# A graph network on one core: the node jobs of the background all ahead of its slot jobs, one every four groups

## The chip, the cores and the metric

The kernel runs on one core of one Trainium2 chip. The metric is device time in microseconds (us) of one execution, the median of the runs shown. PE is TensorE (PEld its weight loads), DVE is VectorE, ACT is ScalarE, POOL is GpSimd and SP is SyncE, which here only issues DMAs. L12 is line 12 of the kernel before; in the changed kernel the same code stands up to seven lines lower.

## The reference

50,000 nodes have 96 features each, and 25,000 edges join them. The edges are sorted by `dst`. Four layers follow one another, each under a residual sum and a layer norm:

```python
edge_index = jnp.stack([src, dst])
x = _layernorm(x + _L0(x, edge_index, edge_attr_17, ...))   # edge network, sum over dst
x = _layernorm(x + _L1(x, edge_index))                      # K = 10 times: out = spmm(out) * 0.9 + h * 0.1
x = _layernorm(x + _L2(x, edge_index))                      # K = 16 times: normalized sum over neighbours
x = _layernorm(x + _L3(x, edge_index, W1, b1, W2, b2, prelu_a))  # twice: x @ W, sum, + b, prelu
```

Most rows of the result hang on few edges or on none. A node without edges needs in layer 3 only its own row: two products with the 96x96 weights, two prelus and a norm.

## The kernel before, in words

**The passes.** After a preparation of some 1,280 us, `passes` runs four stages: "power" (layer 1, K1 = 10 passes), "smooth" (layer 2, K2 = 16 passes), and the two convolutions "conv1" and "conv2" of one pass each. A pass handles the 25,088 edge slots in NGP = 49 groups of 512 rows. For each group g POOL issues four indirect DMAs of 128 rows each (the gathers, L1823) into one of RG = 7 buffers `l_g`. PE transposes them (`turn`, L1850), DVE runs the segmented sum over the 512 columns (`scan`, L2007), PE turns the sums of group g - 2 back (`turn_back`, L1876 in power; L1858 and L1867 in smooth), DVE makes the new rows (L2050 and L2059 or L2063 in power; L2032 and L2050 in smooth), and SP stores them in a table (L2228). In the first pass of power and of smooth ACT scales the gathered rows first (`prepare`, L1922), and PE's `turn` waits for that. In power's ninth pass (p = 8) DVE does three operations in place of the one of L2063 (L2070, L2071, L2072).

**What POOL waits for.** Ahead of the gathers of group q it waits until PE's step q - 7 is done, since they write that group's buffer, and until the gathers of group q - 2 have landed. Ahead of a pass it waits until every row of the pass before is stored. In that gap it does other work where there is some: in power passes 2 to 9 up to 25 gathers of other rows (L1806), and in smooth a lot of finished rows.

**The background.** Beside power and smooth runs a second, independent piece of work, the class `Tail`: layer 3 for nodes and slots that need no neighbours. It has 149 jobs: 100 node jobs (500 nodes each, 125 rows on the partitions, loaded from `x3d`, stored in the output) and 49 slot jobs (512 slots each, loaded from `x3t`, stored in `outc` and partly in `h1t`). A job is a chain over all engines, and each of its links stands at a fixed offset. `background` calls `turn` once for each group 1 to 40 of every pass but a stage's last. These calls are the "slots", 40 a pass, 360 in power and 600 in smooth; slot s stands at group s % 40 + 1, on PE ahead of that group's own `turn`, on DVE and ACT behind that group's own work. A job that begins at slot b has:

- SP loads the rows at b (L227) and stores the result at b + 12
- PE transposes at b + 1 (L253); ACT copies at b + 2 (L261); PE multiplies at b + 3 (L266); ACT rectifies at b + 4 (L274, L275); DVE merges at b + 5 (L280); PE multiplies at b + 6 (L289); ACT rectifies at b + 7 (L307, L308); DVE merges at b + 8 (L314, L316); PE transposes back at b + 9 (L326)
- DVE takes the statistics at b + 10 (L338 to L345), ACT their root at b + 10 (L353); DVE inverts at b + 11 (L363, L364), ACT scales the rows at b + 11 (L373)

Each link waits on a semaphore for the one before. All queues run in order, so an engine that waits for a link holds back what is behind it, the work of the pass too. `PERIOD` = 6: job n begins at slot 6n. The order of the jobs is 60 node jobs, 49 slot jobs, 40 node jobs.

**The lots.** The rows that the slot jobs stored are scattered to the output in 19 lots of 2 to 4 groups, four indirect DMAs each group (`send_lot`, L1780). SP loads a lot into one of two tiles, of which the second is `lots[1]`. One lot goes out ahead of each smooth pass 1 to 15, two behind smooth's last gathers and two behind conv1's. A lot of 2 groups is 8 scatters, one of 3 groups 12.

Of the kernel before, what the change touches and what calls it, by code (L numbers as in the profile page):

```python
# [46 lines left out]
PERIOD = 6  # L47
# [66 lines left out]
class Tail:  # L114


    def __init__(self, prog, s):
# [11 lines left out]
        self.up, self.down = tmp("up", [D, GE]), tmp("down", [D, GE])  # L129
# [138 lines left out]
    def rectify_first(self, act, n):  # L268
        w = U * self.parts(n)
        self.seen(act, n, 3)  # L270
        if n:
            self.seen(act, n - 1, 9)
        a, z = self.nc.scalar, self.p.bank[5][0:D, 0:w]
        a.activation(self.up[:, 0:w], z, ACT.Relu, bias=self.p.c1[:, 0:1])  # L274
        a.activation(self.down[:, 0:w], z, ACT.Relu, bias=self.p.c1n[:, 0:1], scale=-1.0).then_inc(self.rect1, 1)  # L275

    def merge_first(self, dve, n):
        w = U * self.parts(n)
        dve.wait_ge(self.rect1, n + 1)
        self.nc.vector.scalar_tensor_tensor(out=self.up[:, 0:w], in0=self.down[:, 0:w], scalar=self.p.neg[:, 0:1],  # L280
                                            in1=self.up[:, 0:w], op0=ALU.mult, op1=ALU.add).then_inc(self.merged1, 1)

    def mult_second(self, pe, n):
# [2007 lines left out]
```

## Time and profile before

| | |
|---|---|
| time, median of 3 runs | 9357.71 us (9357.03 to 9362.42) |
| the profiled execution, span | 9366.9 us |
| PE busy | 5546.5 us (59%), 23638 instructions |
| DVE busy | 4843.1 us (52%) |
| ACT busy | 2149.1 us (23%) |
| POOL busy | 6850.8 us (73%), 7074 instructions |
| DMA | 957.89 MB, mean 102 GB/s |
| mean granted TensorE clock | 0.635 of full speed |

Power's first gather starts at 1284.8 us, smooth's at 4337.0 us, conv1's at 8571.1 us. The groups of instructions give for each line its count, its busy time, the mean of one, and the idle time of the engine ahead of it with what ended it; the timeline gives single instructions in order of time. An instruction behind "x4" is four in a row, given with their common length. PE's times are those of a pipeline, so one instruction may start before the other's end.

### The profile page before, as it was taken

How to read it: one execution, taken by the hardware profiler on the slowest of the kernel's cores; microseconds unless marked ns; L12 is line 12 of the kernel's file. 1: busy time of each engine (PE TensorE's matmuls, PEld its weight loads, DVE VectorE, ACT ScalarE, POOL GpSimd, SP SyncE). 2: the span in 40 equal slices, each digit the busy share in tenths (PEclk: the TensorE clock that was granted, in tenths of full speed). 3: DMA queues.
4: the chain of work that ended last, by engine and by line, in shares of the span. 5: the costliest groups of instructions: out<-in, count | busy, mean ns of one | idle time of the engine just before them, and what ended most of it. 6: DMA issues, size and time to landing. Idle time of an engine off the chain costs nothing. (4 is left out here: it accounts for less than half of the span.)

```text
span 9366.9 us, 86355 instructions
## 1 busy us (share of the span) xinstructions
PE 5546.5 (59%) x23638; PEld 4458.1 (48%) x23638; DVE 4843.1 (52%) x12040; ACT 2149.1 (23%) x5791; POOL 6850.8 (73%) x7074
## 2 busy tenths in 40 slices
PE   7565754444443444313777777777777777676643
PEld 6455642233222232202665666656555665555643
DVE  7666644454444456643555555555555554455454
ACT  2366542011000011331211111111111110046433
POOL 6554767777777777767777777777777777777777
PEclk9655655555555555556777777777777777666565
DMA  7555353343333343432444444444444443333311
GB/s 144 130 166 162 80 97 96 98 107 98 97 97 96 98 106 97 111 83 70 112 107 109 114 112 108 110 109 104 104 105 102 107 108 97 94 96 87 90 46 37
DMA packets 909306, 957.89 MB, mean 102 GB/s; under 512 B 370946, under 2 KB 799320, under 8 KB 908726
## 3 DMA queue, kind: packets, MB, share of 16 engines
q1 hardware_dynamic: 652854, 588.49, 20.9%
q0 software_dynamic: 225792, 323.35, 18.3%
q10 hardware_dynamic: 30178, 40.53, 1.2%
q8 instruction: 191, 3.13, 0.1%
q14 instruction: 291, 2.38, 0.1%
HBM read 561.02 MB, written 418.54 MB: 105 GB/s over the span
## 5 line engine op out<-in xcount | busy, mean ns | idle before, releaser
L1823 POOL DMA_INDIRECT l_g<-tab,l x2940 | 2844.3, 967 | 917.0 <-issue 865.7
L2007 DVE TENSOR_TENSOR_SCAN l_w<-l_m,l_w,bank 96x512 f32<-96x512 bf16 x1248 | 1592.3, 1276 | 2890.7 <-PE bank L1850 2884.8
L1850 PE MATMUL bank<-ident,l_g 128*96 128x128 f32 x5096 | 1200.2, 381 | 2368.9 <-DMA l_g<-tab,XM 1080.2
L1850 PEld LDWEIGHTS bank<-ident,l_g 128*96 128x96 f32 x5096 | 780.5, 174 | 2858.4 <-DMA l_g<-tab,XM 1207.0
L1823 POOL DMA_INDIRECT l_g<-tab,XM x1764 | 1723.6, 977 | 550.0 <-issue 511.5
L1867 PEld LDWEIGHTS bank<-ident,l_w 96*128 96x128 f32 x6272 | 1602.9, 328 | 324.2 <-issue 253.4
L1867 PE MATMUL bank<-ident,l_w 96*128 96x96 f32 x6272 | 1505.2, 400 | 8.2 <-DVE l_w L2007 7.9
L1858 PE MATMUL bank<-XM,ident 128*128 128x384 f32 x1568 | 921.6, 681 | 0.0
L353 ACT ACTIVATE tail_sc<-tail_mv,eps_x 125x4 f32<-125x4 f32 (+1 forms) x149 | 44.3, 297 | 3404.5 <-DVE tail_mean L345 3404.5
L1876 PE MATMUL bank<-ident,l_w 96*128 96x96 f32 x1960 | 412.1, 364 | 43.2 <-DVE l_w L2007 43.1
L2050 DVE TENSOR_TENSOR T<-T,coef_d 128x384 f32<-128x384 f32 x735 | 412.2, 561 | 25.3
L2032 DVE TENSOR_TENSOR T<-bank,T 128x384 f32<-128x384 f32 x784 | 416.2, 531 | 3.3 <-PE bank L1867 0.2
L1876 PEld LDWEIGHTS bank<-ident,l_w 96*128 96x128 f32 x1960 | 365.2, 228 | 60.7 <-DVE l_w L2007 55.9
L289 PE MATMUL bank<-tail_up,v 96*96 96x500 f32 (+1 forms) x298 | 254.4, 951 | 219.1 <-DVE tail_up L280 219.1
L1858 PEld LDWEIGHTS bank<-XM,ident 128*128 128x128 f32 x1568 | 343.8, 271 | 4.4
L326 PE MATMUL bank<-ident,tail_up 96*125 96x96 f32 (+1 forms) x596 | 138.5, 376 | 290.9 <-DVE tail_up L316 290.9
L373 ACT ACTIVATE tail_y<-bank,tail_of,tail_sc 125x96 f32<-125x96 f32 (+1 forms) x596 | 208.7, 431 | 442.7 <-DVE tail_of L364 442.7
L923 POOL DMA_INDIRECT meta_s<-meta,src_i x196 | 190.6, 972 | 109.0 <-DVE junk_n L991 54.7
L2007 DVE TENSOR_TENSOR_SCAN l_w<-l_m,bank 96x512 f32<-96x512 bf16 x26 | 31.6, 1217 | 456.3 <-PE bank L1850 435.2
L326 PEld LDWEIGHTS bank<-ident,tail_up 96*125 96x125 f32 (+1 forms) x596 | 105.0, 250 | 323.9 <-DVE tail_up L316 323.9
L2050 DVE TENSOR_TENSOR l_o<-bank,XM 128x384 f32<-128x384 f32 x490 | 258.3, 529 | 1.3 <-DVEq L2074 0.2
L1793 POOL DMA_INDIRECT T<-tab,own x196 | 188.5, 962 | 92.6 <-issue 59.4
(309 smaller groups left out, 9858.8 us busy)
## 6 DMA issues: line engine op xcount, KB each, us to landing
tab<-T SPq DMA_DIRECT2D x784, 192.0 KB, 2.4
tab<-l_o SPq DMA_DIRECT2D x441, 192.0 KB, 2.9
l_m<-mask_d SPq DMA_DIRECT2D x784, 96.0 KB, 2.8
l_m<-mask_s SPq DMA_DIRECT2D x490, 96.0 KB, 2.8
l_g<-tab,l POOLq DMA_INDIRECT x2940
l_g<-tab,XM POOLq DMA_INDIRECT x1764
x3t<-XM SPq DMA_DIRECT2D x98, 192.0 KB
x_meta<-in_x_dram SPq DMA_DIRECT2D x25, 750.0 KB
```

Source lines behind the costliest of these rows:

```text
L289: self.nc.tensor.matmul(z, self.p.v2[0:D, :], self.up[:, 0:w], start=True, stop=True)
L326: self.nc.tensor.transpose(self.p.bank[7][0:R, u * D:(u + 1) * D], self.up[:, u * R:(u + 1) * R], self.p.ident[0:D, 0:D])
L373: last = self.nc.scalar.activation(self.Y[n % 2][0:R, c], self.p.bank[7][0:R, c], ACT.Identity, bias=self.of[n % 2][0:R, u:u + 1], scale=s ...
L923: nc.gpsimd.indirect_dma_start(out=into[:, t, :], out_offset=None, in_=of_, in_offset=bass.IndirectOffsetOnAxis(ap=index[:, t:t + 1], axis=0),
L1823: nc.gpsimd.indirect_dma_start(out=tile(G[q % RG], t), out_offset=None, in_=tables[0:table_at + (2 - p % 2) * TR, :] if p else first, in_o ...
L1850: last = nc.tensor.transpose(a_bank(q)[0:D, u:GE:U], G[q % RG][:, u * D:(u + 1) * D], self.ident[:, :])
L1858: nc.tensor.matmul(b_bank(q)[:, 0:GD], self.ident[:, :], group(XS, q % NGP), start=True, stop=False, skip_group_check=True)
L1867: last = nc.tensor.matmul(b_bank(q)[:, u * D:(u + 1) * D], W[q % RW][:, u:GE:U], self.ident[0:D, 0:D], start=False, stop=True, skip_group_ ...
L1876: last = nc.tensor.transpose(b_bank(q)[:, u * D:(u + 1) * D], W[q % RW][:, u:GE:U], self.ident[0:D, 0:D])
L2007: v.tensor_tensor_scan(out=W[q % RW][:, :], data0=masks[q % RM][:, :], data1=a_bank(q)[0:D, :], initial=W[(q - 1) % RW][:, GE - 1:GE] if q ...
L2032: v.tensor_tensor(out=there, in0=b, in1=there, op=ALU.add).then_inc(summed.sem, 1)
L2050: v.tensor_tensor(out=o, in0=of, in1=by[:, at].unsqueeze(2).to_broadcast([P, U, D]), op=ALU.mult).then_inc(made.sem, 1)
```

## The change

- The order of the jobs is now 100 node jobs, then 49 slot jobs. Node jobs begin every 4 slots (`NODE_PERIOD`), slot jobs every 6 (`SLOT_PERIOD`). So node job n begins at slot 4n (the last at 396), and the first slot job at slot 402. The 360 slots of power hold 90 node jobs (before: 60); smooth pass 0 holds the other 10. Slot jobs run from smooth pass 1 to pass 8; behind that there is no background (before: up to pass 13).
- The tiles `up` and `down`, through which a job passes, get a second copy for odd node jobs. It lies in the second lot tile, which holds no lot so long. A rectify waits for the end of the job two before, no longer one, where both are node jobs.
- The lots are 18 in place of 19: sizes 2, 3, 2, 3, ... and then 4, 3, 4, 3. The first goes out ahead of smooth pass 2 (before: pass 1), the later ones ahead of each pass as before. The 196 scatters stay 196.
- The offsets of the links within a job, the slots, the passes and all else stay.

```diff
-PERIOD = 6
+NODE_PERIOD, SLOT_PERIOD = 4, 6
...
-LOTS = (2,) * 10 + (3,) * 5 + (3, 4, 3, 4)
+LOTS = (2, 3) * 7 + (4, 3, 4, 3)
...
-AHEAD = 60
...
-        self.jobs = nodes[:AHEAD] + slots + nodes[AHEAD:]
+        self.jobs = nodes + slots
         self.count = len(self.jobs)
+        first_slot = (len(nodes) - 1) * NODE_PERIOD + SLOT_PERIOD
+        self.begin = [n * NODE_PERIOD for n in range(len(nodes))] + [first_slot + n * SLOT_PERIOD for n in range(NGP)]
+        self.at_slot = {slot: n for n, slot in enumerate(self.begin)}
...
-        self.up, self.down = tmp("up", [D, GE]), tmp("down", [D, GE])
+        spare = prog.lots[1]
+        self.up, self.down = ([tmp(n, [D, GE]), spare[0:D, k * GE:(k + 1) * GE]] for k, n in enumerate(("up", "down")))
...
         def due(offset):
-            n, r = divmod(slot - offset, PERIOD)
-            return n if r == 0 and 0 <= n < self.count else None
+            return self.at_slot.get(slot - offset)
...
+    def copy(self, n):
+
+        return 0 if self.slots(n) else n % 2
...
         self.seen(act, n, 3)
-        if n:
-            self.seen(act, n - 1, 9)
+        before = n - 1 if self.slots(n - 1) else n - 2
+        if before >= 0:
+            self.seen(act, before, 9)
```

ACT's queue in the first pass of power. `l_g` are the gathered rows, `tail_...` and, as the second copy, `lot` are tiles of the background. Before:

```order
L1922 ACTIVATE l_g<-l_g,XM 128x96 x8
L353 ACTIVATE tail_sc<-tail_mv,eps_x 125x4
L274 ACTIVATE tail_up<-bank,c 96x500
L275 ACTIVATE tail_down<-bank,c1n 96x500
L1922 ACTIVATE l_g<-l_g,XM 128x96 x4
L373 ACTIVATE tail_y<-bank,tail_of,tail_sc 125x96 x4
L1922 ACTIVATE l_g<-l_g,XM 128x96 x8
L307 ACTIVATE tail_up<-bank,c 96x500
L308 ACTIVATE tail_down<-bank,c2n 96x500
L1922 ACTIVATE l_g<-l_g,XM 128x96 x4
L261 ACTIVATE tail_xt<-bank 96x500
```

The same place in the changed kernel:

```order
L1929 ACTIVATE l_g<-l_g,XM 128x96 x8
L360 ACTIVATE tail_sc<-tail_mv,eps_x 125x4
L267 ACTIVATE tail_xt<-bank 96x500
L1929 ACTIVATE l_g<-l_g,XM 128x96 x4
L380 ACTIVATE tail_y<-bank,tail_of,tail_sc 125x96 x4
L314 ACTIVATE lot<-bank,c 96x500
L315 ACTIVATE lot<-bank,c2n 96x500
L1929 ACTIVATE l_g<-l_g,XM 128x96 x4
L281 ACTIVATE tail_up<-bank,c 96x500
L282 ACTIVATE tail_down<-bank,c1n 96x500
```

The copy (L267) now stands right behind the root (L360), and the second rectify (L314, L315) behind the scaling (L380), in the same slot; before, each had another slot than these.

DVE's queue in a middle pass of power, before:

```order
L314 SCALAR_TENSOR_TENSOR tail_up<-tail_down,neg,tail_up 96x500
L316 TENSOR_TENSOR tail_up<-tail_up,tail_xt 96x500
L2007 SCALAR_TENSOR_TENSOR l_w<-l_m,l_w,bank 96x512
L2050 TENSOR_TENSOR l_o<-bank,XM 128x384
L2063 TENSOR_TENSOR T<-T,l_o 128x384
L2007 SCALAR_TENSOR_TENSOR l_w<-l_m,l_w,bank 96x512
L2050 TENSOR_TENSOR l_o<-bank,XM 128x384
L2063 TENSOR_TENSOR T<-T,l_o 128x384
L338 BN_STATS tail_stat<-bank 125x6 x4
```

And in the changed kernel, from the same operation on:

```order
L321 SCALAR_TENSOR_TENSOR lot<-lot,neg 96x500
L323 TENSOR_TENSOR lot<-lot,tail_xt 96x500
L2014 SCALAR_TENSOR_TENSOR l_w<-l_m,l_w,bank 96x512
L2057 TENSOR_TENSOR l_o<-bank,XM 128x384
L2070 TENSOR_TENSOR T<-T,l_o 128x384
L287 SCALAR_TENSOR_TENSOR tail_up<-tail_down,neg,tail_up 96x500
L2014 SCALAR_TENSOR_TENSOR l_w<-l_m,l_w,bank 96x512
L2057 TENSOR_TENSOR l_o<-bank,XM 128x384
L2070 TENSOR_TENSOR T<-T,l_o 128x384
L345 BN_STATS tail_stat<-bank 125x6 x4
```

The first merge of the next job (L287) now stands in the group between the second merge and the statistics: each group of a node stretch has one piece of background on DVE, where before three of six had none.

## Rows read from the trace of the kernel before

**Rows 1.** The page: span.

```profile
span 9366.9 us, 86355 instructions
```

**Rows 2.** Groups of instructions: busy, mean ns of one | idle before, releasers.

```profile
L1823 POOL DMA_INDIRECT l_g<-tab,l x2940 | 2844.3, 967 | 917.0 <-issue 865.7 <-DMA l_g<-tab,l 36.2 <-PE bank L1850 7.6
```

**Rows 3.** Timeline, power pass 4: start us, us, engine, line [idle before <-releaser].

```profile
2560.09 0.33 SPq L227 DMA_DIRECT2D tail_x<-x3d  x1
...
2565.32 1.07 PE L253 MATMUL bank<-ident,tail_x 125*96 125x125 f32 x4 [0.72 <-DMA tail_x<-x3d]
...
2568.38 0.58 ACT L261 ACTIVATE tail_xt<-bank 96x500 f32<-96x500 f32 x1 [3.14 <-PE bank L1850]
...
2572.32 1.28 DVE L2007 TENSOR_TENSOR_SCAN l_w<-l_m,l_w,bank 96x512 f32<-96x512 bf16 x1 [1.75 <-PE bank L1850]
...
2574.43 0.73 DVE L314 SCALAR_TENSOR_TENSOR tail_up<-tail_down,neg,tail_up 96x500 f32<-96x500 f32 x1
...
2575.93 1.15 PE L326 MATMUL bank<-ident,tail_up 96*125 96x96 f32 x4 [3.00 <-DVE tail_up L316]
...
2576.87 1.88 PE L266 MATMUL bank<-tail_xt,v 96*96 96x500 f32 x2
...
2579.64 1.28 DVE L2007 TENSOR_TENSOR_SCAN l_w<-l_m,l_w,bank 96x512 f32<-96x512 bf16 x1 [3.77 <-PE bank L1850]
...
2582.48 1.28 DVE L2007 TENSOR_TENSOR_SCAN l_w<-l_m,l_w,bank 96x512 f32<-96x512 bf16 x1 [0.62 <-PE bank L1850]
...
2583.76 0.94 POOL L1823 DMA_INDIRECT l_g<-tab,XM  x1 [0.30 <-issue]
...
2585.79 0.17 DVE L345 TENSOR_SCALAR tail_mean<-tail_mv 125x4 f32<-125x4 f32 x1
2585.99 0.30 ACT L353 ACTIVATE tail_sc<-tail_mv,eps_x 125x4 f32<-125x4 f32 x1 [17.03 <-DVE tail_mean L345]
...
2588.18 1.28 DVE L2007 TENSOR_TENSOR_SCAN l_w<-l_m,l_w,bank 96x512 f32<-96x512 bf16 x1 [2.23 <-PE bank L1850]
...
2590.49 0.16 DVE L364 TENSOR_TENSOR tail_of<-tail_mean,tail_sc 125x4 f32<-125x4 f32 x1
2590.57 0.73 DVE L280 SCALAR_TENSOR_TENSOR tail_up<-tail_down,neg,tail_up 96x500 f32<-96x500 f32 x1
2590.69 1.40 ACT L373 ACTIVATE tail_y<-bank,tail_of,tail_sc 125x96 f32<-125x96 f32 x4 [3.28 <-DVE tail_of L364]
...
2594.23 0.67 ACT L307 ACTIVATE tail_up<-bank,c 96x500 f32<-96x500 f32 x1 [2.13 <-PE bank L1850]
...
2594.80 0.66 ACT L308 ACTIVATE tail_down<-bank,c2n 96x500 f32<-96x500 f32 x1
```

**Rows 4.** Timeline, first pass of power: ACT and PE behind it.

```profile
1415.63 1.16 ACT L1922 ACTIVATE l_g<-l_g,XM 128x96 f32<-128x96 f32 x4
1416.85 1.09 PE L1850 MATMUL bank<-ident,l_g 128*96 128x128 f32 x4 [5.49 <-ACT l_g L1922]
```

**Rows 5.** Timeline of DVE, power pass 8.

```profile
3640.21 1.28 DVE L2007 TENSOR_TENSOR_SCAN l_w<-l_m,l_w,bank 96x512 f32<-96x512 bf16 x1
...
3643.88 0.18 DVE L363 RECIPROCAL tail_sc<-tail_sc 125x4 f32<-125x4 f32 x1 [0.24 <-DVE T L2072]
...
3651.48 1.28 DVE L2007 TENSOR_TENSOR_SCAN l_w<-l_m,l_w,bank 96x512 f32<-96x512 bf16 x1 [0.24 <-DVE T L2072]
...
3655.10 1.28 DVE L2007 TENSOR_TENSOR_SCAN l_w<-l_m,l_w,bank 96x512 f32<-96x512 bf16 x1 [0.24 <-DVE T L2072]
```

**Rows 6.** Timeline, smooth pass 0.

```profile
4433.14 0.60 PE L1850 MATMUL bank<-ident,l_g 128*96 128x128 f32 x4
...
4433.78 1.28 DVE L2007 TENSOR_TENSOR_SCAN l_w<-l_m,l_w,bank 96x512 f32<-96x512 bf16 x1 [1.08 <-PE bank L1850]
...
4436.02 0.75 DVE L338 BATCH_NORM_STATS2 tail_stat<-bank 128x6 f32<-128x96 f32 x4
...
4440.03 1.09 PE L1850 MATMUL bank<-ident,l_g 128*96 128x128 f32 x4 [3.93 <-ACT l_g L1922]
...
4442.19 1.98 PE L1867 MATMUL bank<-ident,l_w 96*128 96x96 f32 x8
```

**Rows 7.** Timeline of POOL between smooth passes 2 and 3.

```profile
5110.47 0.94 POOL L1823 DMA_INDIRECT l_g<-tab,l  x1 [0.30 <-issue]
...
5124.36 0.99 POOL L1823 DMA_INDIRECT l_g<-tab,l  x1 [2.68 <-issue]
```

**Rows 8.** Timeline of POOL, power pass 4: a gather beside DVE's L280.

```profile
2590.01 1.18 POOL L1823 DMA_INDIRECT l_g<-tab,XM  x1 [0.30 <-issue]
```

More of the change, by code:

```diff
@@ L55 @@
 LOT_ROOM = (4, 3)
-LOTS = (2,) * 10 + (3,) * 5 + (3, 4, 3, 4)
-LOT_SENT = {"smooth": tuple((p, 0) for p in range(1, 16)) + ((15, 49),) * 2, "conv1": ((0, 49),) * 2}
-LOT_LOADED = {"smooth": tuple((p, 42) for p in range(15)) + ((15, 12), (15, 24)), "conv1": ((0, 8), (0, 20))}
-AHEAD = 60
+LOTS = (2, 3) * 7 + (4, 3, 4, 3)
+LOT_SENT = {"smooth": tuple((p, 0) for p in range(2, 16)) + ((15, 49),) * 2, "conv1": ((0, 49),) * 2}
+LOT_LOADED = {"smooth": tuple((p, 42) for p in range(1, 15)) + ((15, 12), (15, 24)), "conv1": ((0, 8), (0, 20))}
 EPS = 1e-5
@@ L196, in seen @@
     def seen(self, eng, n, offset):
-        slot, base, passes = n * PERIOD + offset, 1, K1 - 1
+        slot, base, passes = self.begin[n] + offset, 1, K1 - 1
         if slot >= passes * SLOTS:
@@ L214, in jobs_to @@
     def jobs_to(self, group):
-        return AHEAD + group
+        return NJ // U + group
     def place(self, nodes, slots, n):
@@ L270, in rectify_first @@
         self.seen(act, n, 3)
-        if n:
-            self.seen(act, n - 1, 9)
+        before = n - 1 if self.slots(n - 1) else n - 2
+        if before >= 0:
+            self.seen(act, before, 9)
         a, z = self.nc.scalar, self.p.bank[5][0:D, 0:w]
-        a.activation(self.up[:, 0:w], z, ACT.Relu, bias=self.p.c1[:, 0:1])
-        a.activation(self.down[:, 0:w], z, ACT.Relu, bias=self.p.c1n[:, 0:1], scale=-1.0).then_inc(self.rect1, 1)
+        a.activation(self.up[self.copy(n)][:, 0:w], z, ACT.Relu, bias=self.p.c1[:, 0:1])
+        a.activation(self.down[self.copy(n)][:, 0:w], z, ACT.Relu, bias=self.p.c1n[:, 0:1], scale=-1.0).then_inc(self.rect1, 1)
     def merge_first(self, dve, n):
@@ L279, in merge_first @@
         dve.wait_ge(self.rect1, n + 1)
-        self.nc.vector.scalar_tensor_tensor(out=self.up[:, 0:w], in0=self.down[:, 0:w], scalar=self.p.neg[:, 0:1],
-                                            in1=self.up[:, 0:w], op0=ALU.mult, op1=ALU.add).then_inc(self.merged1, 1)
+        self.nc.vector.scalar_tensor_tensor(out=self.up[self.copy(n)][:, 0:w], in0=self.down[self.copy(n)][:, 0:w], scalar=self.p.neg[:, 0:1],
+                                            in1=self.up[self.copy(n)][:, 0:w], op0=ALU.mult, op1=ALU.add).then_inc(self.merged1, 1)
     def mult_second(self, pe, n):
@@ L288, in mult_second @@
         z = self.p.bank[6][0:D, 0:w]
-        self.nc.tensor.matmul(z, self.p.v2[0:D, :], self.up[:, 0:w], start=True, stop=True)
+        self.nc.tensor.matmul(z, self.p.v2[0:D, :], self.up[self.copy(n)][:, 0:w], start=True, stop=True)
         if not self.slots(n):
@@ L294, in mult_second @@
         for u in range(U):
-            self.nc.tensor.transpose(self.p.bank[7][0:R, u * D:(u + 1) * D], self.up[:, u * R:(u + 1) * R],
+            self.nc.tensor.transpose(self.p.bank[7][0:R, u * D:(u + 1) * D], self.up[self.copy(n)][:, u * R:(u + 1) * R],
                                             self.p.ident[0:D, 0:D])
@@ L306, in rectify_second @@
             a.activation(self.H[:, :], self.p.bank[7][:, 0:GD], ACT.Copy).then_inc(self.h1_kept, 1)
-        a.activation(self.up[:, 0:w], z, ACT.Relu, bias=self.p.c2[:, 0:1])
-        a.activation(self.down[:, 0:w], z, ACT.Relu, bias=self.p.c2n[:, 0:1], scale=-1.0).then_inc(self.rect2, 1)
+        a.activation(self.up[self.copy(n)][:, 0:w], z, ACT.Relu, bias=self.p.c2[:, 0:1])
+        a.activation(self.down[self.copy(n)][:, 0:w], z, ACT.Relu, bias=self.p.c2n[:, 0:1], scale=-1.0).then_inc(self.rect2, 1)
     def merge_second(self, dve, n):
@@ L312, in merge_second @@
         dve.wait_ge(self.rect2, n + 1)
-        up, v = self.up[:, 0:w], self.nc.vector
-        self.link(dve, v.scalar_tensor_tensor(out=up, in0=self.down[:, 0:w], scalar=self.p.neg[:, 0:1], in1=up,
+        up, v = self.up[self.copy(n)][:, 0:w], self.nc.vector
+        self.link(dve, v.scalar_tensor_tensor(out=up, in0=self.down[self.copy(n)][:, 0:w], scalar=self.p.neg[:, 0:1], in1=up,
                                               op0=ALU.mult, op1=ALU.add))
@@ L325, in join @@
         for u in range(U):
-            self.nc.tensor.transpose(self.p.bank[7][0:R, u * D:(u + 1) * D], self.up[:, u * R:(u + 1) * R],
+            self.nc.tensor.transpose(self.p.bank[7][0:R, u * D:(u + 1) * D], self.up[self.copy(n)][:, u * R:(u + 1) * R],
                                             self.p.ident[0:D, 0:D])
```

## The prediction, made blind

> **What bounds the kernel now.** I read the page first: POOL is busy 73% of the span of 9366.9 us [rows 1], more than any other engine, and its gathers fill all of power and smooth. Next the groups of instructions: 2,940 gathers take 967 ns each, and the idle time ahead of them is 917 us, of which 866 us is "issue", 312 ns apiece, and only 44 us is a wait for another engine or a landing [rows 2]. So POOL runs at its own pace, 967 + 312 = 1,279 ns a gather, 5.12 us a group, 20.5 us for four groups. All that PE, DVE and ACT do, the background included, is hidden as long as PE's step q - 7 is done when POOL comes to group q. How much room that leaves is in the timeline [rows 3]: the last gather of one group ends at 2583.76 + 0.94 = 2584.70, and DVE starts the scan of that group at 2588.18, when PE's step is done, 3.5 us later. POOL asks for that step six groups later: the room is 6 x 5.12 + 0.3 - 3.5 = 27.5 us. That is the number the change is measured against: a background that delays PE by less costs nothing, each us beyond is a us of the span.
>
> **What is only moved.** The count of jobs, matmuls, DVE and ACT operations, loads, stores and scatters stays. 30 node jobs move from smooth to power, and smooth pass 0 holds 10 node jobs. At POOL's pace their place is indifferent. The second copy of `up` and `down` has the same shapes, and no link of the chain is shortened by it: it lifts a wait that the offsets already keep.
>
> **The new ring.** The offsets stay while the distance falls from 6 slots to 4, so links of jobs n, n - 1 and n - 2 now meet in one slot. On DVE, slots 0 to 3 of each four have the second merge, first merge, statistics, inversion. ACT has in slot 2 the root and, behind it, the next job's copy; in slot 3 the scaling and, behind it, the second rectify. PE multiplies in slots 2 and 3, and in slot 1 it transposes back and forth. Each waits for the one before, and closes on itself after four slots. I add it up for a middle pass of power, from the start of DVE's scan in slot 1 [rows 3]:
> - DVE's own work takes 2574.43 - 2572.32 = 2.11, the first merge (L280) 0.73: 2.84
> - PE's product and `turn`: L280 ends at 2591.30, PE's step is done at 2594.23, 2.93: 5.77 (slot 2)
> - own work and statistics, 2582.48 to 2585.96, 3.48: 9.25
> - root 0.30, copy 0.58, with their starts 0.9: 10.15
> - product and `turn` again, 2.93: 13.1 (slot 3)
> - own work and inversion, 2588.18 to 2590.65, 2.47: 15.55
> - scaling 1.40 and second rectify, 2594.23 to 2595.46, 1.23: 18.2
> - second merge until PE starts, 2574.43 to 2575.93, 1.50: 19.7 (slot 0)
> - transposes back 0.94 (2575.93 to 2576.87), the next job's 1.07, `turn` 1.1: 22.8 (slot 1 of the next four)
>
> So the ring takes 22.8 us where POOL takes 20.5. With 6 slots (30.7 us) no such ring closes: the copy stands alone in its slot, and so does the second rectify. In the new order PE falls behind by 2.3 us a job. A pass holds ten jobs, nine turns of the ring: 21 us, and 2.9 more inside a turn (13.1 against two groups, 10.2), 24 us in all. That is under 27.5. In the eight groups without slots DVE needs some 2.2 us a group, so PE wins back 8 x 2.9 = 23 us. **Power passes 1 to 7: 0**, by a margin of 3.5 us.
>
> One wait stands close beside: the rows' load takes 2565.32 - 2560.09 = 5.2 us [rows 3]. SP comes to it when DVE has made the rows of slot 3, at about 15.2, so it lands at 20.4, and PE wants it at 20.6.
>
> **Power pass 0.** Here ACT also scales the gathered rows, 1.16 us a group, and PE's `turn` waits for it [rows 4]. It stands behind the second rectify, so `turn` of slot 0 ends at 18.2 + 1.2 + 1.1 = 20.5, DVE's own work at 22.6, the second merge at 24.1, and the ring at 27. With DVE's slightly shorter own work there I take 26.7, 6.2 us behind a turn. The first jobs must fill the pipeline; seven full turns give 43, the inside of a turn 3, less the room of 27.5 - 1.2: **+20 us** (10 to 30).
>
> **Power pass 8.** DVE's own work takes 3643.88 - 3640.21 = 3.67, 1.56 more [rows 5]. That counts in slots 1, 2, 3, and in slot 0 DVE, free at 20.2, comes to the merge at 23.9: the ring is 28.5. 8 us a turn, nine turns, 72; 6 inside a turn; less 27.5: **+50 us** (35 to 60). Then the end: PE is 27.5 us late, DVE needs 3655.10 - 3651.48 = 3.62 a group [rows 5], so eight groups win back 12. The last rows are stored some 16 us late, and pass 9 has no other gathers left to hide it: **+16 us** (10 to 20).
>
> **Smooth pass 0.** DVE's own work is 4436.02 - 4433.78 = 2.24, `turn_back` keeps PE until 4444.17, 3.05 us behind a `turn` that ends at 4441.12 [rows 6], and ACT scales here too. The same sum: 2.97 and PE free at 3.05; 6.0; 9.6; 10.5; 13.4; 16.0; 18.7; scaling 19.9; `turn` 21.0; merge 24.8; ring 27.9. This holds at TensorE's lower clock. `turn` takes 1.09 us behind a wait of 3.93 us, and 0.60 in a run of PE work [rows 6]: 1.2 and 2.4 GHz. All at the higher one, four `turn`s save 2 us, two products some 2, the other transposes 1: 23. The ring has waits on PE and busy runs; I take 26: 5.5 x 9 + 3 - 26.3 = **+27 us** (0 to 44). The last groups, at 3.5 us each, win back 13 of 26, and no lot stands behind this pass now: **+13 us** (5 to 20).
>
> The Trainium skill ("TensorE: Matmul & The Clock Gate", Part 1) has the clock set by how busy the array has been of late. By that rule a denser background could itself lift the clock in power; the row with 3.93 us of wait and 1.09 agrees with its other half. What that would give is the rival "clock" below.
>
> **Lots.** Between two passes the rows' stores take until 5124.36 where the last gather ended at 5111.41: 12.9 us with 8 scatters under it and a rest of 2.68 [rows 7]; other such gaps need less. So 8 scatters, 10.2 us, are hidden, and of 12, 15.3 us, some 3 to 4 stick out. The change has two such lots more, and ahead of pass 1 an empty gap of the same length: **+8 us** (4 to 8).
>
> **Sum.** 20 + 50 + 16 + 27 + 13 + 8 = 134 us on the span of 9366.9 us [rows 1], 9501. The median of the runs, 9357.7, lies 9 us under the span; both shift alike: **9492 us**.
>
> **Rivals.**
> - *The middle passes break too* (0.20). If a turn takes 1.1 us more, for instance as the load lands late behind SP's stores, it is 23.9: 3.4 x 9 + 3 - 27.5 = 6 us in each of seven passes: 9534. For it: the margin is 3.5 us. Against: a lag ahead of the first jobs is nil.
> - *The clock rises* (0.15). With PE at 2.4 GHz in the ring every turn of it loses 3 to 4 us: power pass 0 and smooth 0 stay within the room, pass 8 costs 5 x 9 + 6 - 27.5 = 22 and 10 at its end, lots 8: 9398. For it: PE is busier; against: in the turns of power it waits three times.
> - *The ring stays slack* (0.07): the offsets already separate what depends, so only the lots stand: 9366.
> - *Faster* (0.03). A gather takes 1.18 us where DVE's L280, from 2590.57 to 2591.30, falls on it [rows 3, 8], 0.24 more than 0.94 [rows 3]. A job has three such merges, up to 0.7 us of POOL, 107 us in all. Where two merges fall on one gather, or on a POOL that waits, they cost once or nothing. If the denser jobs saved a quarter so and PE stayed within its room, 9357.7 - 27 + 8 = 9339. It decides if the ring takes under 20.5 us. The Trainium skill ("SBUF — State Buffer", "Who interferes with whom") says that a DVE instruction with two SBUF inputs contends with a GpSimd instruction that reads SBUF; the row agrees.
>
> **How the numbers follow.** The forecast has 0.55. It is likely slower by over 0.2% (about 19 us, what a measurement of this kernel can tell from no change) in it and in the first two rivals: 0.90; within 0.2% by the slack ring: 0.07; faster: 0.03. The low ends sum to 10 + 35 + 10 + 0 + 5 + 4 = 64 (9422), the high ends to 30 + 60 + 20 + 44 + 20 + 8 = 182, and the middle passes at 6 us each 224 (9582). To take in part of the clock's case the range begins at 9400: 9400 to 9580.
>
> **What would show it.** In the changed trace POOL's gathers should wait for PE's L1857 (today's L1850), by tens of us, in power passes 0 and 8 and in smooth pass 0, in steps of one turn of the ring, and hardly elsewhere. Power's last gap should be near 27 us, and the one behind smooth pass 0 near 25. In power passes 1 to 7 PE should start a group's transposes up to 20 us behind the landing towards slot 40, and be level again at the next pass. ACT's copy should start right behind the root in every fourth slot. If POOL never waits, the ring is wrong; if it waits in passes 1 to 7, my turn is too short or the room smaller than 27.5 us.

## The result, and the profile after

| | before | after |
|---|---|---|
| time, median of 4 runs | 9357.4 us | 9532.4 us (9519.4 to 9543.4) |
| the profiled execution, span | 9366.9 us | 9517.6 us |
| mean granted TensorE clock | 0.635 | 0.626 |

The change makes the kernel slower: the ratio is 1.0187 (95% interval 1.0173 to 1.0200), 175 us between the medians. The forecast was 9492, with a range of 9400 to 9580. The profiled execution of after is the fastest of its four runs and that of before lies above the median of its own, so the two traces differ by less, 150.7 us. After's trace also has a preparation 8.4 us shorter, which the change doesn't touch. From power's first gather on after is thus 159 us longer, and that is what the rows below account for.

The page of after, and its groups of instructions; they answer to [rows 1, 2]:

```profile
span 9517.6 us, 86351 instructions
...
L1830 POOL DMA_INDIRECT l_g<-tab,l x2940 | 2835.9, 965 | 933.3 <-issue 865.8 <-DMA l_g<-tab,l 30.8 <-DMA tab<-T 27.6
...
L1830 POOL DMA_INDIRECT l_g<-tab,XM x1764 | 1758.6, 997 | 614.2 <-issue 514.6 <-DMA l_g<-tab,XM 51.4 <-PE bank L1857 48.2
```

The second group as it was before:

```profile
L1823 POOL DMA_INDIRECT l_g<-tab,XM x1764 | 1723.6, 977 | 550.0 <-issue 511.5 <-DMA l_g<-tab,XM 37.6 <-PE bank L1850 0.9
```

The first group, the gathers of smooth passes 1 to 15, is almost as it was. The second is that of power passes 1 to 9. A gather takes 997 ns there where it took 977, and PE now ends 48.2 us of POOL's idle time.

**Where POOL waits.** The same group in one pass, here power pass 8 of after (3593 to 3889 us), then smooth pass 0 (4444 to 4731):

```profile
L1830 POOL DMA_INDIRECT l_g<-tab,XM x196 | 194.7, 994 | 100.6 <-issue 49.7 <-PE bank L1857 41.8 <-DMA l_g<-tab,XM 9.1
```

```profile
L1830 POOL DMA_INDIRECT l_g<-tab,first_i x196 | 190.2, 970 | 95.6 <-issue 48.6 <-PE bank L1857 41.6 <-DMA l_g<-tab,first_i 5.5
```

Before, both passes have 59.7 us of idle time (these rows of before follow), so after waits 41 and 36 us longer.

```profile
L1823 POOL DMA_INDIRECT l_g<-tab,XM x196 | 192.2, 980 | 59.7 <-issue 56.1 <-DMA l_g<-tab,XM 2.7 <-PE bank L1850 0.9
...
L1823 POOL DMA_INDIRECT l_g<-tab,first_i x196 | 190.6, 972 | 59.7 <-issue 55.1 <-DMA l_g<-tab,first_i 2.4 <-PE bank L1850 2.1
```

Power pass 0, before and after. The idle time ahead of its first gather, 32.1 and 31.1 us, is in these rows and not in the pass; without it the pass has 61.8 and 74.1 us, so it waits 12.4 us longer.

```profile
L1823 POOL DMA_INDIRECT l_g<-x1t,XM x196 | 187.6, 957 | 93.9 <-issue 90.8 <-DMA l_g<-x1t,XM 2.8 <-PE bank L1850 0.3
...
L1830 POOL DMA_INDIRECT l_g<-x1t,XM x196 | 190.8, 974 | 105.2 <-issue 82.9 <-PE bank L1857 12.8 <-DMA l_g<-x1t,XM 9.5
```

**The ring at work.** One turn in power pass 8 of after, from scan to scan, 3759.42 to 3787.10 us, 27.7 us (answers to [rows 5]):

```profile
3759.42 1.27 DVE L2014 TENSOR_TENSOR_SCAN l_w<-l_m,l_w,bank 96x512 f32<-96x512 bf16 x1 [2.93 <-PE bank L1857]
3759.65 0.94 POOL L1830 DMA_INDIRECT l_g<-tab,XM  x1 [2.34 <-PE bank L1857]
...
3764.37 0.30 ACT L360 ACTIVATE tail_sc<-tail_mv,eps_x 125x4 f32<-125x4 f32 x1 [16.37 <-DVE tail_mean L352]
3764.57 0.56 ACT L267 ACTIVATE tail_xt<-bank 96x500 f32<-96x500 f32 x1
...
3765.19 1.98 PE L272 MATMUL bank<-tail_xt,v 96*96 96x500 f32 x2 [5.17 <-ACT tail_xt L267]
...
3768.30 0.94 POOL L1830 DMA_INDIRECT l_g<-tab,XM  x1 [3.96 <-PE bank L1857]
...
3772.09 1.40 ACT L380 ACTIVATE tail_y<-bank,tail_of,tail_sc 125x96 f32<-125x96 f32 x4 [6.96 <-DVE tail_of L371]
...
3773.37 0.67 ACT L314 ACTIVATE tail_up<-bank,c 96x500 f32<-96x500 f32 x1
...
3777.03 1.16 PE L333 MATMUL bank<-ident,tail_up 96*125 96x96 f32 x4 [6.91 <-DVE tail_up L323]
...
3780.14 0.94 POOL L1830 DMA_INDIRECT l_g<-tab,XM  x1 [1.81 <-DMA l_g<-tab,XM]
...
3787.10 1.27 DVE L2014 TENSOR_TENSOR_SCAN l_w<-l_m,l_w,bank 96x512 f32<-96x512 bf16 x1 [2.93 <-PE bank L1857]
3787.34 0.94 POOL L1830 DMA_INDIRECT l_g<-tab,XM  x1 [2.34 <-PE bank L1857]
```

The copy L267 had its input long ago and stands behind the root L360, which came to an ACT idle for 16.37 us. PE waited 5.17 us for that copy. The second rectify L314 stands behind the scaling L380 in the same way, and PE 6.91 us for what follows from it. POOL then waits for PE's step, and the pattern (2.34, 3.96, 1.81) comes back with every turn.

In the middle of power (passes 1 to 7) the ring closes too, but POOL hardly waits. One turn of pass 4, from scan to scan, 2587.52 to 2609.92, 22.40 us (answers to [rows 3, 8]):

```profile
2587.52 1.27 DVE L2014 TENSOR_TENSOR_SCAN l_w<-l_m,l_w,bank 96x512 f32<-96x512 bf16 x1 [3.73 <-PE bank L1857]
...
2592.57 0.73 DVE L321 SCALAR_TENSOR_TENSOR tail_up<-tail_down,neg,tail_up 96x500 f32<-96x500 f32 x1 [0.45 <-ACT tail_down L315]
...
2594.07 1.16 PE L333 MATMUL bank<-ident,tail_up 96*125 96x96 f32 x4 [4.50 <-DVE tail_up L323]
...
2596.95 1.27 DVE L2014 TENSOR_TENSOR_SCAN l_w<-l_m,l_w,bank 96x512 f32<-96x512 bf16 x1 [2.94 <-PE bank L1857]
2597.64 1.24 POOL L1830 DMA_INDIRECT l_g<-tab,XM  x1 [0.30 <-DMA l_g<-tab,XM]
...
2598.60 0.54 DVE L2070 TENSOR_TENSOR T<-T,l_o 128x384 f32<-128x384 f32 x1
...
2599.06 0.73 DVE L287 SCALAR_TENSOR_TENSOR lot<-lot,neg 96x500 f32<-96x500 f32 x1
2599.18 1.43 POOL L1830 DMA_INDIRECT l_g<-tab,XM  x1 [0.30 <-issue]
...
2599.84 1.98 PE L296 MATMUL bank<-lot,v 96*96 96x500 f32 x2 [2.29 <-DVE lot L287]
...
2600.91 0.94 POOL L1830 DMA_INDIRECT l_g<-tab,XM  x1 [0.30 <-issue]
...
2607.05 1.98 PE L272 MATMUL bank<-tail_xt,v 96*96 96x500 f32 x2 [3.73 <-ACT tail_xt L267]
...
2609.92 1.27 DVE L2014 TENSOR_TENSOR_SCAN l_w<-l_m,l_w,bank 96x512 f32<-96x512 bf16 x1 [3.73 <-PE bank L1857]
```

**The gathers themselves are longer.** The second thing to see there is a gather of 1.43 us beside the first merge L287, and one of 1.24 beside L2070, the pass's own sum of two tiles, where the undisturbed one takes 0.94. All 1,372 gathers of power passes 1 to 7, before and after:

```profile
L1823 POOL DMA_INDIRECT l_g<-tab,XM x1372 | 1345.2, 980 | 419.9 <-issue 389.3 <-DMA l_g<-tab,XM 30.6
```

```profile
L1830 POOL DMA_INDIRECT l_g<-tab,XM x1372 | 1376.5, 1003 | 427.6 <-issue 383.2 <-DMA l_g<-tab,XM 38.0 <-PE bank L1857 6.4
```

Busy time grows by 31.3 us and idle time by 7.7: 39 us in seven passes for which the forecast had 0. Counted one by one, the gathers that take over 0.98 us exceed 0.944 by 50 us in all before and by 82 after. Those with a background merge beside them hold 21 of the 50 and 42 of the 82, the others 29 and 40.

**The gaps.** POOL's first gather of power pass 9, then that of smooth pass 1:

```profile
3915.37 1.14 POOL L1830 DMA_INDIRECT l_g<-tab,XM  x1 [26.56 <-issue]
...
4754.99 0.94 POOL L1830 DMA_INDIRECT l_g<-tab,l  x1 [24.58 <-DMA tab<-T]
```

Before they were 11.0 and 11.5 us. The account from the starts and ends of all passes, in us: waits and gathers of power pass 0, 15.5; passes 1 to 7, 39.0; pass 8, 43.5; the gap ahead of pass 9, 15.5; pass 9 and the other gaps of power, 2.8; smooth pass 0, 35.5; the gap behind it, 13.1; the lots' gaps, 7.8; smooth passes 1 to 15, which have 33 jobs less, -12.7; what follows smooth's last gather, -0.9. Sum 159.1.

### The profile page after: what moved, and what is told of

Its sections match the earlier page's. It is cut to its first block and busy times, and to the rows that moved or that the text cites. A ratio compares the mean times of both kernels' runs of the same rounds, so it can differ in the third digit from the quotient of the medians.

```text
span 9517.6 us, 86351 instructions
## 1 busy us (share of the span) xinstructions
PE 5643.3 (59%) x23638; PEld 4518.2 (47%) x23638; DVE 4834.8 (51%) x12040; ACT 2121.3 (22%) x5791; POOL 6878.8 (72%) x7074
## 5 line engine op out<-in xcount | busy, mean ns | idle before, releaser
L1830 POOL DMA_INDIRECT l_g<-tab,XM x1764 | 1758.6, 997 | 614.2 <-issue 514.6
L1857 PEld LDWEIGHTS bank<-ident,l_g 128*96 128x96 f32 x5096 | 813.6, 177 | 2384.0 <-DMA l_g<-tab,l 1082.6
L1865 PE MATMUL bank<-XM,ident 128*128 128x384 f32 x1568 | 959.4, 707 | 0.0
L360 ACT ACTIVATE tail_sc<-tail_mv,eps_x 125x4 f32<-125x4 f32 (+1 forms) x149 | 44.3, 297 | 3007.8 <-DVE tail_mean L352 3007.8
L272 PE MATMUL bank<-tail_xt,v 96*96 96x500 f32 (+1 forms) x298 | 277.6, 1033 | 358.9 <-ACT tail_xt L267 358.9
L1939 ACT ACTIVATE T<-T,both_d 128x96 f32<-128x96 f32 x196 | 57.0, 362 | 1755.6 <-DVE T L2039 1755.0
L380 ACT ACTIVATE tail_y<-bank,tail_of,tail_sc 125x96 f32<-125x96 f32 (+1 forms) x596 | 208.2, 429 | 656.5 <-DVE tail_of L371 656.5
L1830 POOL DMA_INDIRECT l_g<-x1t,XM x196 | 190.8, 974 | 105.2 <-issue 82.9
L1830 POOL DMA_INDIRECT l_g<-tab,first_i x196 | 190.2, 970 | 95.6 <-issue 48.6
```

Of the source, the lines that this page charges most:

```text
L272: self.nc.tensor.matmul(self.p.bank[5][0:D, 0:w], self.p.v1[0:D, :], self.xt[n % 2][:, 0:w], start=True, stop=True)
L380: last = self.nc.scalar.activation(self.Y[n % 2][0:R, c], self.p.bank[7][0:R, c], ACT.Identity, bias=self.of[n % 2][0:R, u:u + 1], scale=s ...
L1830: nc.gpsimd.indirect_dma_start(out=tile(G[q % RG], t), out_offset=None, in_=tables[0:table_at + (2 - p % 2) * TR, :] if p else first, in_o ...
L1857: last = nc.tensor.transpose(a_bank(q)[0:D, u:GE:U], G[q % RG][:, u * D:(u + 1) * D], self.ident[:, :])
L1865: nc.tensor.matmul(b_bank(q)[:, 0:GD], self.ident[:, :], group(XS, q % NGP), start=True, stop=False, skip_group_check=True)
L1939: last = a.activation(x, x, ACT.Copy, scale=by[:, t:t + 1])
```

## The experiments

All have before beside them on the same chip, and each ratio is taken against it. Two things were to be told apart: what the ring costs, and what the merges' effect on the gathers costs.

### The order on ACT

Slot by slot, ACT's queue gets the rectifies and the copy ahead of the scaling and the root, in after.

```diff
-        if kind == "act" and n is not None:
-            self.normal(eng, n)
-        n = due(10)
-        if kind == "act" and n is not None:
-            self.root(eng, n)
-        n = due(11)
...
         n = due(2)
         if kind == "act" and n is not None:
             self.lift(eng, n)
+        n = due(11)
+        if kind == "act" and n is not None:
+            self.normal(eng, n)
+        n = due(10)
+        if kind == "act" and n is not None:
+            self.root(eng, n)
```

> The changed kernel with one edit: on ACT a job's root and scaling stand behind the rectifies and the copy of the same slot, no longer ahead of them. Nothing else moves. Theory (a ring over PE, DVE and ACT longer than POOL's four groups, and a room of 27.5 us): the copy no longer waits for the statistics, the second rectify no longer for the inversion; by the rows of before the ring of four slots is 18.7 us in the middle of power (22.4 measured in the changed kernel), 24.4 in power pass 0 (25.9), 24.6 in power pass 8 (27.7), 25 in smooth pass 0 (up to 27.3). So POOL's waits within those three passes fall from 15, 41 and 36 us to about 3, 12 and 16, the gaps behind passes 8 and smooth 0 stay near 25 us, and PE's lateness in power passes 1 to 7, up to 20 us now, is gone. Time about 60 us under the changed kernel, some 95 us over the kernel before. Rival (the loss is DVE's and POOL's contention or the mere density of the jobs): the same operations run in the same passes, so nothing changes.

Measured: 9436.9 us, ratio 1.0082 (1.0066 to 1.0099), some 95 us less than after, where 60 less was expected. The longer waits of power 0, power 8 and smooth 0 are gone (0.2, 0.9 and 0.7 us), and not only smaller as expected. One turn in power pass 8, timeline of ACT and DVE:

```profile
3702.87 1.28 DVE L2014 TENSOR_TENSOR_SCAN l_w<-l_m,l_w,bank 96x512 f32<-96x512 bf16 x1
3702.97 0.30 ACT L360 ACTIVATE tail_sc<-tail_mv,eps_x 125x4 f32<-125x4 f32 x1 [11.57 <-DVE tail_mean L352]
3703.18 0.66 ACT L314 ACTIVATE lot<-bank,c 96x500 f32<-96x500 f32 x1
...
3714.72 0.58 ACT L267 ACTIVATE tail_xt<-bank 96x500 f32<-96x500 f32 x1 [5.30 <-PE bank L1857]
...
3726.77 1.28 DVE L2014 TENSOR_TENSOR_SCAN l_w<-l_m,l_w,bank 96x512 f32<-96x512 bf16 x1
```

The turn takes 23.9 us and no longer 27.7, and the copy L267 waits for PE alone. It follows that the order of ACT's queue, a late link of one job ahead of an early link of the next, twice in a turn, is what makes the ring 27.7 long. In smooth pass 0 the clock helped too: 0.70 of full speed here, 0.62 in after. What doesn't go away are the two gaps (24.1 and 24.8 us): at 23.9 a turn PE is still late when POOL has done, though never late enough to hold it. Nor does the excess of power 1 to 7: its passes take 253.9 to 258.5 us, 1795 in all, against 1763 before and 1802 in after, though their turns are down from 22.4 to some 21 us.

### One SBUF input for the merges, in after and in before

The second input of each merge comes from a PSUM bank instead of SBUF, with the shape as it was. The background's rows are then not what the reference has, and the time of everything else can be read.

```diff
         self.nc.vector.scalar_tensor_tensor(out=self.up[self.copy(n)][:, 0:w], in0=self.down[self.copy(n)][:, 0:w], scalar=self.p.neg[:, 0:1],
-                                            in1=self.up[self.copy(n)][:, 0:w], op0=ALU.mult, op1=ALU.add).then_inc(self.merged1, 1)
+                                            in1=self.p.bank[6][0:D, 0:w], op0=ALU.mult, op1=ALU.add).then_inc(self.merged1, 1)
...
-        v.tensor_tensor(out=up, in0=up, in1=self.xt[n % 2][:, 0:w], op=ALU.add).then_inc(self.merged2, 1)
+        v.tensor_tensor(out=up, in0=up, in1=self.p.bank[6][0:D, 0:w], op=ALU.add).then_inc(self.merged2, 1)
```

> The changed kernel with the second input of a job's three merges on DVE (L287, L321, L323) taken from a PSUM bank in place of the SBUF tiles up and xt; so the background's rows are wrong, all counts, sizes and waits are as they were. Question: power passes 1 to 7 take some 6 us more each than before with no wait of POOL, as more gathers take 1.2 us in place of 0.94. Theory (port: a DVE instruction with two SBUF inputs holds up the gather beside it): the long gathers of these passes fall from 39 to about 15 or 20 and each pass is back at 250 to 252 us, 40 us in all; the ring is as long as before, so the waits in power passes 0 and 8 and smooth pass 0 stay or grow by a few us. About 45 us under the changed kernel. Rival (the denser loads and stores of the background make gathers long): no change.

> The edit of one_sbuf_2 in the kernel before (merges L280, L314, L316 with one SBUF and one PSUM input; the background's rows are wrong). Theory (port, but by the phase at which DVE's operations meet a gather): in the kernel before the passes with background are no slower than the groups without it, so the merges cost little there: 0 to 40 us less in all. If the price were fixed per merge, it would be 149 jobs x 3 x some 0.1 to 0.24 us, 45 to 107 us. Rival (DMA traffic): no change.

Measured: after with it 9438.3 us, ratio 1.0089 (1.0072 to 1.0106), 94 us less than after where 45 was expected; before with it 9320.3 us, ratio 0.9954 (0.9940 to 0.9968), some 41 us less where 0 to 40 was. The 1,372 gathers of power passes 1 to 7, first after's, then before's:

```profile
L1830 POOL DMA_INDIRECT l_g<-tab,XM x1372 | 1307.4, 953 | 425.5 <-issue 372.2 <-DMA l_g<-tab,XM 39.6 <-PE bank L1857 13.6
```

```profile
L1823 POOL DMA_INDIRECT l_g<-tab,XM x1372 | 1327.9, 968 | 419.4 <-issue 378.7 <-DMA l_g<-tab,XM 32.8 <-PE bank L1850 7.9
```

With the merges off SBUF's second input, after's gathers lose 69 us (1376.5 to 1307.4) with 70 jobs beside them, before's 17 us (1345.2 to 1327.9) with 47. Passes 1 to 7 of after then take 245.9 to 248.7 us, less than before's own. So the excess of the forecast's empty term is gathers made longer by DVE, and the ring isn't needed for it: with one SBUF input the turns of power 1 to 7 still take 22.5 us. The ring stays in the other passes too: its turns take 25.9 and 27.7 us in power 0 and 8, and POOL's waits there even grow to 22 and 47 us, as a faster POOL reaches PE sooner. In smooth pass 0 they fall from 36 to 24 us. There the turns are shorter (24.2 to 26.4 us), and the granted clock of that stretch was higher in this run, 0.71 where after had 0.62:

```profile
4377.50:4649.00 271.50, 187.77 (x196) 0.71 0.37 95
```

Without the merges' second SBUF input the change costs 9438.3 - 9320.3 = 118 us (126 by the two ratios), with it 175. So 49 to 57 us of the result hang on that input, up to 12 of them perhaps on the clock of smooth pass 0 instead. The rest is ring, gaps and lots, of which the forecast had 134.

Per job the merges' second input costs 1.0 us in after and 0.4 in before, since two things change with it. The gathers with a merge beside them lose their excess, 42 us in after and 21 in before (above). And in both edited kernels every gather that is still over 0.98 us, 69 of them in after and 123 in before, stands beside the pass's own L2070 (before: L2063), a tensor_tensor with two SBUF inputs. These hold 13 and 33 us, where the long gathers without a merge held 40 and 29. After thus loses another 27 us at that line, and before gains 4. That the edit shifts where L2070 falls on the gathers would explain it, but no run holds that apart.

### A ring of six buffers

After with RG = 6, so that POOL waits one group sooner.

```diff
-RG = 7
+RG = 6
```

> The changed kernel with 6 gather buffers in place of 7: POOL asks for PE's step five groups later, the room is one group (5.1 us) less. Theory: POOL's waits within power pass 0, power pass 8 and smooth pass 0 grow by about 5 us each (15, 41, 36 to 20, 46, 41), and the gaps behind power pass 8 and smooth pass 0 (26.6 and 24.6 us) shrink by about 5 each, since PE is less late when POOL ends; power passes 1 to 7, where PE is up to 20 us late against a room of 22.4, still hardly wait. In all about 5 us slower than the changed kernel. Rival (POOL waits for something else than PE's step q - 7): the waits stay or grow everywhere alike.

Measured: 9519.9 us, ratio 1.0168 (1.0151 to 1.0185). The 5 us more that were expected are not there; against after's 1.0187 (1.0173 to 1.0200) the time can't be told apart. The waits and gaps are as expected. Over the 0.30 us of issue ahead of each gather POOL waits 23.8, 46.7 and 44.6 us in power 0, power 8 and smooth 0, where it was 14.8, 41.0 and 35.9, and the gaps behind power 8 and smooth 0 shrink from 26.6 and 24.6 to 21.7 and 18.8. The room of the buffers is a store of lateness: what POOL doesn't wait for within the pass it waits for at its end, since the pass ends when its last rows are stored. Power 1 to 7 wait 0.5 to 3.3 us a pass: even with some 5 us less room they hold. So the room is not what makes those passes longer.

### The longer distance where the ring is slowest

After with a distance of 6 slots in power pass 0, power pass 8 and smooth pass 0; the slot jobs then begin later, and so do the lots.

```diff
-        self.begin = [n * NODE_PERIOD for n in range(len(nodes))] + [first_slot + n * SLOT_PERIOD for n in range(NGP)]
+        self.begin = [0]
+        while len(self.begin) < len(nodes):
+            self.begin.append(self.begin[-1] + (SLOT_PERIOD if self.begin[-1] // SLOTS in (0, 8, 9) else NODE_PERIOD))
...
-LOTS = (2, 3) * 7 + (4, 3, 4, 3)
+LOTS = (3,) * 9 + (2,) * 4 + (3, 4, 3, 4)
```

> The changed kernel with node jobs 6 slots apart in power passes 0 and 8 and smooth pass 0, and 4 apart elsewhere; the first slot job then begins at slot 442, so the lots go out from smooth pass 3 on (nine of 3 groups, four of 2, then 3, 4, 3, 4). Queues and offsets are those of the changed kernel. Theory (ring against room, pass by pass): the waits of POOL go where the distance is 6 again: 15, 41 and 36 us to about 2, 0 and 0, the gaps behind power pass 8 and smooth pass 0 from 26.6 and 24.6 back to 11 and 12. Power passes 1 to 7 stay at 257 us each (257.4 in the changed kernel). Smooth pass 1 now has ten node jobs at distance 4 but no scaling on ACT; its ring is 24.4 us at TensorE's lower clock: 0 to 10 us of waits and a gap up to 10 us longer. A second gap without a lot and larger lots cost some 8 us more. About 95 us under the changed kernel, 1.008 of the kernel before. Rival (nodes first is slow wherever they stand): the loss moves to the passes that got the jobs and the time stays at 1.019.

Measured: 9408.1 us, ratio 1.0056 (1.0039 to 1.0073), 124 us less than after, where some 95 less was expected. Its waits in the three passes are 3.8, 0.0 and 0.6 us, the gaps 17.2 and 11.5. What is left of the change are above all passes 1 to 7. They take 255.3 to 256.6 us each:

```profile
L1833 POOL DMA_INDIRECT l_g<-tab,XM x1372 | 1368.2, 997 | 425.8 <-issue 381.5 <-DMA l_g<-tab,XM 36.7 <-PE bank L1860 7.6
```

That is 23 us of longer gathers and 6 of idle time over before's row above, plus 6 us of the gap ahead of pass 9, and 13 us of smooth's gaps, nine of which now hold 12 scatters where before five did. The three slow places and the middle of power are separate costs.

### A background without both costs

In the last three kernels PE adds the bias through a row of ones, ACT rectifies once, and DVE merges that with PE's result from PSUM. This is the same function in another form: a job has one operation with two SBUF inputs and not three, two ACT operations less, and its first merge stands one slot earlier. First on before, then on after with the order on ACT from above, then that with a distance of 6 in power pass 8. The core of the edit, in after's form:

```diff
-        a.activation(self.up[self.copy(n)][:, 0:w], z, ACT.Relu, bias=self.p.c1[:, 0:1])
-        a.activation(self.down[self.copy(n)][:, 0:w], z, ACT.Relu, bias=self.p.c1n[:, 0:1], scale=-1.0).then_inc(self.rect1, 1)
+        a.activation(self.down[self.copy(n)][0:D, 0:w], z, ACT.Relu, scale=-1.0).then_inc(self.rect1, 1)
...
-                                            in1=self.up[self.copy(n)][:, 0:w], op0=ALU.mult, op1=ALU.add).then_inc(self.merged1, 1)
+                                            in1=self.p.bank[5][0:D, 0:w], op0=ALU.mult, op1=ALU.add).then_inc(self.merged1, 1)
```

> The kernel before with another form of a job's two prelus: the bias comes out of the matmul (a row of ones under xt and up), ACT writes only relu(-y), and DVE adds (1 - a) times that to y straight from PSUM. So the merges L280 and L314 have one SBUF input, ACT has two activations less a job, and the first merge stands one slot earlier. L316 keeps two SBUF inputs. Theory (port): in before_one_sbuf_2 all three merges with one SBUF input gave 43 us; two of three give about 30: 9330 us, ratio 0.9965 (0.9945 to 0.998). Rival (only L316's place counts, or ones and bias cost PE time): 1.0.

> The changed kernel with both: ACT's order of act_order_2 and the prelus of v_before. Theory: against act_order_2 (1.008) contention falls by two thirds of what one_sbuf_2 took off the changed kernel (92 us): 60 us. The ring no longer goes through the first merge in slot 1; summed as before it is 21 us in power pass 8 (23.9 measured in act_order_2) and 22.4 in power pass 0 (23.6), so PE is level at the end of pass 8 and the gap behind it falls from 24 to about 12 us; the gap behind smooth pass 0 stays near 20 to 25. Together 1.008 - 0.0065 - 0.0013 = 1.0003 (0.998 to 1.003) of the kernel before. Rival (savings do not add up): 1.005.

> v_after with node jobs 6 slots apart in power pass 8 alone (first slot job at slot 416, lots as in the changed kernel). Theory: by then the ring there is inside the room, so this is worth little: power pass 8 takes some 3 to 5 us less by fewer gathers held up, the rest is as v_after: 0 to 8 us less. If v_after's gap behind pass 8 is still over 20 us, it falls to 11.

| | time, us | ratio to before |
|---|---|---|
| new merges on before | 9326.1 | 0.9961 (0.9947 to 0.9975) |
| new merges and order on after | 9359.4 | 1.0001 (0.9991 to 1.0010) |
| the same, distance 6 in power 8 | 9350.1 | 0.9992 (0.9983 to 1.0002) |

The 1,372 gathers, of the first and of the second kernel:

```profile
L1826 POOL DMA_INDIRECT l_g<-tab,XM x1372 | 1329.4, 969 | 419.4 <-issue 375.5 <-DMA l_g<-tab,XM 35.1 <-PE bank L1853 8.8
```

```profile
L1833 POOL DMA_INDIRECT l_g<-tab,XM x1372 | 1341.5, 978 | 423.4 <-issue 384.7 <-DMA l_g<-tab,XM 34.1 <-PE bank L1860 4.6
```

The first is faster than both kernels, and it keeps before's distances. Which of its three differences (inputs, ACT's operations, the earlier merge) makes it faster was not tried apart; 15.8 us of the gathers' busy time in power passes 1 to 7 are gone, of some 36 us in all. The time of the second came as expected, that of the third can't be told from it by the two intervals. Between the first two kernels lie 33 us, with the ring gone (turns of some 20 us in power 8, gap behind it 10.8 us). In the traces 16 of them are longer middle passes (12 of busy time and 4 of idle time in these two rows), and 9 the gap behind smooth 0, now 22.0 us. So even the change that is rid of its ring wins nothing here: the background was hidden before, and in each form tried the denser one was slower.

## Why the prediction was right, and where it was off

- **What bounds the kernel**: right. POOL's gathers set the pace, and all that counts is what holds them or stretches them.
- **The ring's sum**: right, nearly link by link. The middle of power was given 22.8 us and took 22.40. Along [rows 3]'s links, first merge done, product and `turn`, statistics, root and copy: 2.84, 5.77, 9.24 and 10.10 us behind the scan of slot 1, where the sum has 2.84, 5.77, 9.25 and 10.15. Power 0 was given 26.7 and took 25.9; power 8 28.5 and 27.7; smooth 0 26, and 27.3 in its second half.
- **Power 0 and 8**: +20 and +50 said, waits of +12.4 and +41 measured. The term that was mis-sized is the turn: 0.8 us too much, over seven and nine turns, 6 and 7 us.
- **Smooth 0**: +27 said, +36 measured. The step "all four at the higher clock 23, I take 26" took too much of the higher clock. It is the mis-sized term of this pass. The stretches of the pass show the granted clock, before and after, at 0.75 and 0.62 of full speed (the column behind the count of gathers; the first row is before's):

```profile
4337.00:4588.00 251.00, 190.56 (x196) 0.75 0.42 110
```

```profile
4444.00:4731.00 287.00, 190.17 (x196) 0.62 0.35 90
```

  And in a turn of its second half PE's `turn`s take 1.06 us, near the 1.09 that [rows 6] show at 1.2 GHz, and not the 0.60 of 2.4 GHz:

```profile
4649.06 1.06 PE L1857 MATMUL bank<-ident,l_g 128*96 128x128 f32 x4
...
4662.35 1.06 PE L1857 MATMUL bank<-ident,l_g 128*96 128x128 f32 x4
```

  So the sum at the lower clock (27.9) was the nearer end. The Trainium skill ("TensorE: Matmul & The Clock Gate", Part 1) has the clock follow how busy the array was; the traces fit that without deciding it: from the first gather of this pass to that of the next PE has nearly the same number of matmuls (794 before, 806 after), spread over 310 us where it was 261, and the mean granted clock is 0.65 where it was 0.75.

- **The gaps**: +16 and +13 said, +15.5 and +13.1 measured. **Lots**: +8 said, +7.8 measured.
- **The step that failed** is "At POOL's pace their place is indifferent". The contention of the merges stood in the text, as a rival that only saves; that 23 jobs more in power 1 to 7 would bring theirs along was priced at 0. It measured +39 us there, against -12.7 us in smooth, where jobs left. By the count of long gathers 21 of the 39 stand beside merges and 11 beside none; the rest is idle time. The price of the row, 0.24 us a merge or 0.7 a job as an upper end, was also too low for after: 1.0 us a job by the kernel with one SBUF input, L2070's share included.
- **The margin of 3.5 us** in passes 1 to 7 held, and by more than said: PE's lateness (scan's start behind the last gather's end) grows from 2.7 to 20.2 us by slot 40 of pass 4, not by 24. POOL itself was slower, and so drew less far ahead of PE.
- **The rivals**: the middle passes' break gave 9534, close to the time, but by a cause that isn't there: PE ends only 6.4 us of POOL's idle time in those seven passes, and most of the 39 us is busy time. The clock rose a little in the middle of power (0.56 against 0.51 in pass 4), but not where the loss was (0.55 against 0.57 in pass 8, 0.62 against 0.75 in smooth pass 0) nor over the span (0.626 against 0.635). That rival's own sum for pass 8 gives 23.5 us, and not the 22 written. The ring wasn't slack: links of two jobs meet in one slot on ACT, and their order decided. Faster by less contention had the wrong sign: denser jobs cost more of it.
- **The second copy**: "it lifts a wait that the offsets already keep" holds at a distance of 6. At 4 a job's first rectify stands in slot b + 4 and the transposes back of the job before in b + 5, so with one copy it would wait for a step of the next slot. The second copy is what makes the distance possible; no run leaves it out.

The sum of the forecast's own terms is 134 us and the same places measured 131. That the sums agree so well is partly luck: power 0 and 8 were 11 us too high together and smooth 0 8.5 too low. The total hit less well, since 39 - 12.7 + 2 us stand outside, and the median of after lies 13 us above its profiled run.

The Trainium skill ("SBUF — State Buffer", "Who interferes with whom") says that a DVE instruction with two SBUF inputs contends with a GpSimd instruction that reads SBUF. The traces agree for indirect DMAs: with one SBUF input the gathers lose 69 and 17 us, and those that are still long all stand beside L2070 or L2063, which keep two. The same section infers that `tensor_tensor` leaves descriptor generation alone. The timeline differs: in passes 1 to 7 all 70 of the second merges' L323, a plain tensor_tensor, stand beside a gather of over 0.99 us, and none of 70 when one of its inputs is in PSUM.

## What to carry to other kernels

Ask of a denser background not how much work it is but which links of different jobs now meet in one in-order queue: add up the ring that they close from the trace's durations, hold it against the pace of the bounding engine and against the room of the buffers, and expect what the room hides to come back at the end of the pass. Then price what the moved work does to the bounding engine itself: work that is hidden still stretched its instructions here. Where the work is hidden already, look for a form of it that touches less (here one SBUF input), not for another place.

## What the runs showed of the hardware

- **When a two-input merge costs.** Over the timeline of passes 1 to 7 of after, a merge that begins 0.7 to 1.5 us behind a gather's start, so that it runs across the boundary to the next gather, has a long gather (over 0.99 us) beside it in every case: 63 of 63 for L287 and 66 of 66 for L323. Of the 54 L321 (of 70) that begin 0.1 us or less behind a gather's start none has one. So where two merges follow one another at these places, it is mostly the second alone that costs.
- **How much.** In after a long gather beside a merge is 0.10 to 0.50 us over its usual 0.94: mostly 0.49 beside L287 (the 1.43 above), mostly 0.12 beside L323. Before's row had shown 0.24 [rows 8].
- **A ring repeats itself.** In power 8 of after, eight turns in a row took 27.7 us each, with POOL's waits of 2.34 and 3.96 us the same to 0.02. Here waits that come back turn by turn, to the hundredth of a microsecond, were the sign of the ring.
